# Second layer of a two-layer attention and expert kernel: two iterations to a block, six slots, and the experts after the fourth batch

## The reference

```python
xn = _layernorm(x)
q = (xn @ Mq).reshape(B, H, C, K)      # H = 8 heads, K = 64, C = 512
k = (xn @ Mk).reshape(B, H, C, K)
v = (xn @ Mv).reshape(B, H, C, V)      # V = 16
scores = einsum('bhqk,bhck->bhqc', q, k).reshape(B * H, C, C)
att = softmax(scores / sqrt(K), axis=1)            # over the queries
out = einsum('bqhc,bhcd->bqhd', att.reshape(B, C, H, C), v)
# gate: 8 experts, top 1: relu(x @ W1 + b1) @ W2 + b2
x = x + out * silu(experts(xn))
```

## Time and profile before

| | |
|---|---|
| Time, median of 3 runs | 820.05 us (819.98 to 820.12) |
| The profiled execution, its own time | 822.5 us |
| Its span | 820.8 us |
| PE busy (share of the span) | 736.7 us (90%) |
| DVE busy | 579.7 us (71%) |
| ACT busy | 380.4 us (46%) |
| POOL busy | 262.4 us (32%) |
| Second layer's bodies 0 and 1, with 32 scatters | 417.6 to 497.5 us of the span |
| Experts of the second layer | 497.5 to 588.0 us |
| Bodies 2 to 7 and the end | 588.0 to 820.8 us |

### The profile page before, as it was taken

One profiled execution on the slowest core, in us unless ns is written; L12 is line 12 of the kernel. 1 busy time (PEld: TensorE's weight loads), 2 busy tenths in 40 slices (PEclk: granted clock), 3 DMA queues, 4 the chain that ended last, 5 costly groups with the idle time before them and its releaser, 6 DMA issues.

```text
span 820.8 us, 20387 instructions
## 1 busy us (share of the span) xinstructions
PE 736.7 (90%) x6689; PEld 507.2 (62%) x6690; DVE 579.7 (71%) x1525; ACT 380.4 (46%) x922; POOL 262.4 (32%) x404
## 2 busy tenths in 40 slices
PE   5989889999999999994679898999999999999983
PEld 3667677888787787883334347888644444444431
DVE  5888864678777787787487684433587878878772
ACT  2333314444344344342045564444466667777772
POOL 7364200000000000000138743222122246676773
PEclk9999999999999999998599999999999999999996
DMA  8700000000000000000501101222100001111110
GB/s 248 229 0 0 1 1 1 1 1 0 0 0 0 0 0 0 0 0 0 147 15 43 40 21 35 59 58 58 37 2 2 2 15 28 28 28 32 37 33 20
DMA packets 34274, 25.06 MB, mean 31 GB/s; under 512 B 3303, under 2 KB 30626, under 8 KB 34210
## 3 DMA queue, kind: packets, MB, share of 16 engines
q1 hardware_dynamic: 31256, 19.48, 8.2%
q0 software_dynamic: 2048, 4.20, 1.8%
q10 hardware_dynamic: 906, 0.55, 0.3%
HBM read 14.91 MB, written 9.31 MB: 30 GB/s over the span
## 4 chain that ended last, share of the span: by engine, by line
PE 64%; DVE 16%; issue 9%; POOL 4%; ACT 2%; DMA 1%; DVEq 1%; POOLq 0%; ACTq 0%
PE bank L782 12%; PE bank L1345 11%; PE bank L766 9%; PE bank L1330 6%; PE bank L1304 5%; PE bank L1391 4%; PE bank L1400 4%; POOL vs L1256 2%; PE bank L450 1%; POOL xn_all L1270 1%; DVE vt L1533 1%; DMA xn_all<-y_sorted,slot_b 1%; PE bank L809 1%; PE bank L749 1%; DVE acc L1000 1%
## 5 line engine op out<-in xcount | busy, mean ns | idle before, releaser
L1454 ACT ACTIVATE pb<-bank,nmx 128x512 f32<-128x512 f32 x256 | 173.1, 682 | 76.2 <-DVE nmx L1587 73.2
L1587 DVE TENSOR_REDUCE nmx<-bank 128x2 f32<-128x1024 f32 x128 | 156.4, 1222 | 30.4 <-PE bank L1345 28.3
L1345 PE MATMUL bank<-qk 64*128 64x512 f32 x512 | 146.5, 649 | 12.7 <-ACT pb L1454 5.4
L853 ACT ACTIVATE hid<-bank,cols 128x512 f32<-128x512 f32 x128 | 87.9, 687 | 123.3 <-PE bank L766 123.2
L1256 POOL TENSOR_TENSOR vs<-vt,rz 128x256 f32<-128x256 f32 x128 | 78.7, 615 | 135.2 <-DVE rz L1563 120.2
L1330 PEld LDWEIGHTS bank<-pb,vs 128*32 128x32 f32 x2048 | 49.0, 110 | 104.0 <-issue 66.7
L782 PEld LDWEIGHTS bank<-w_e,hid 128*128 128x128 f32 x768 | 98.1, 191 | 8.3 <-DVE acc L1000 1.8
L782 PE MATMUL bank<-w_e,hid 128*128 128x128 f32 x768 | 100.2, 275 | 0.0
L728 POOL TENSOR_TENSOR r<-ve,half_neg 128x4 f32<-128x4 f32 x8 | 8.1, 1010 | 274.1 <-DVE ve L927 274.1
L1330 PE MATMUL bank<-pb,vs 128*32 128x128 f32 x2048 | 84.2, 283 | 6.0 <-POOL vs L1256 5.1
L1345 PEld LDWEIGHTS bank<-qk 64*128 64x128 f32 x512 | 39.3, 187 | 50.7 <-issue 24.3
(11 more groups left out here) (225 smaller groups left out, 1242.2 us busy)
## 6 DMA issues: line engine op xcount, KB each, us to landing
x_sorted<-zero SPq DMA_DIRECT2D x1, 2496.0 KB, 12.3
xn_all<-x_sorted SPq DMA_DIRECT2D x39, 64.0 KB, 1.8
y_sorted<-xn_all SPq DMA_DIRECT2D x39, 64.0 KB, 1.6
x_all<-in_L_attn_x_dram SPq DMA_DIRECT2D x8, 256.0 KB, 6.0
w<-in_L_ffn_W_dram SPq DMA_DIRECT2D x1, 2048.0 KB
out_dram<-xn_all SPq DMA_DIRECT2D x8, 256.0 KB
w_u<-in_L_ffn_ew_dram SPq DMA_DIRECT2D x1, 768.0 KB
w_e<-in_L_ffn_ew_dram SPq DMA_DIRECT2D x1, 768.0 KB
```

What stands on the lines that cost most here:

```text
L853: act.activation(hid[n % NU][:, :], psum[n % NU][:, :], ACT.Gelu, bias=col((ROW_AB1 if n < AC else ROW_EB1 - AC) + n), scale=1.0).then_inc ...
L1345: mm = pe.matmul(psum[score_banks(k) + ab], qk[bt % 2][half, 1, h, 2 * m:2 * m + 2, :].rearrange("p a k -> p (a k)"), qk[bt % 2][half, 0, ...
L1454: act.activation(pb[s + ab][:, :], psum[score_banks(k) + ab], ACT.Exp, bias=nmx[:, s + ab:s + ab + 1], scale=1.0, accum_out=zz[:, s + ab:s ...
L1587: dve.tensor_reduce(nmx[:, s:s + 2], banks[:, score_banks(k):score_banks(k) + 2, :], AX.X, ALU.max, negate=True).then_inc(n_mx, 1)
```

## The change

The line numbers in the changed kernel are up to 8 higher for DVE's lines. `LAG` goes from 3 to 4 and `SLOTS` from 4 to 6; the experts run after four bodies (`BEFORE` 4) and the scatters are spread over twice as many iterations; PE's body goes in blocks of two iterations: two scores, the mixed work of the even iteration, two values, the mixed work of the odd iteration. VAL moves from iteration 6 to 8, two PROJ from 11 and 15 to 10 and 13 (with 13 to 11). DVE stores an even iteration's mixed work after the next maximum and not ahead of it.

```diff
-        LAG = 3
-        SLOTS = 4
+        LAG = 4
+        SLOTS = 6
...
-        MIXED = {1: (PROJ, 0), 3: (PROJ, 1), 4: (TURN, 0), 5: (PROJ, 2), 6: (VAL, 0), 7: (PROJ, 3), 9: (PROJ, 4),
-                 11: (PROJ, 5), 12: (TURN, 1), 13: (PROJ, 6), 15: (PROJ, 7)}
+        MIXED = {1: (PROJ, 0), 3: (PROJ, 1), 4: (TURN, 0), 5: (PROJ, 2), 7: (PROJ, 3), 8: (VAL, 0), 9: (PROJ, 4),
+                 10: (PROJ, 5), 11: (PROJ, 6), 12: (TURN, 1), 13: (PROJ, 7)}
...
-        BEFORE = 2
+        BEFORE = 4
...
-                        for g in range(min(now * 3 // 4, NT), min((now + 1) * 3 // 4, NT)):
+                        for g in range(min(now * 3 // 8, NT), min((now + 1) * 3 // 8, NT)):
...
             def body(bt, kind, last):
-                for i in range(IT):
+                for i in range(0, IT, 2):
                     k = bt * IT + i
                     score(k)
+                    score(k + 1)
+                    mixed(bt, i)
                     if k >= LAG:
                         value(k - LAG)
...
+                        value(k + 1 - LAG)
+                    mixed(bt, i + 1)
...
-                    if i:
+                    if i and i % 2 == 0:
                         mixed(bt, i - 1)
                     if k > 1 and k not in (BEFORE * IT, BEFORE * IT + 1):
                         inverse(k - 2)
...
                     dve.tensor_reduce(nmx[:, s:s + 2], banks[:, score_banks(k):score_banks(k) + 2, :], AX.X, ALU.max,
                                       negate=True).then_inc(n_mx, 1)
+                    if i % 2:
+                        mixed(bt, i - 1)
                 mixed(bt, IT - 1)
```

More of the change, by code:

```diff
@@ L1157, in recurrent_d2_kernel @@
         mixed_bank = lambda u: psum[4 + u % 2] if u < FIRST_USES else psum[6]
-        values_in = lambda bt: 1 if bt == 0 else use_no[bt - 1, 6] + 1
-        pairs_in = lambda bt: FIRST_USES if bt == 0 else use_no[bt - 1, 15] + 1
+        values_in = lambda bt: 1 if bt == 0 else use_no[bt - 1, 8] + 1
+        pairs_in = lambda bt: FIRST_USES if bt == 0 else use_no[bt - 1, 13] + 1
         turn_use = lambda g: LAST_USE if g == 2 * B - 1 else use_no[(g // 2, 12) if g % 2 == 0 else (g // 2 + 1, 4)]
@@ L1355, in _, with mixed @@
                 project(mixed_bank(1 + g), g, 0)
+            def mixed(bt, i):
+                if (bt, i) in use_no:
+                    u = use_no[bt, i]
+                    what, num = MIXED[i]
+                    pe.wait_ge(mb_free, u)
+                    if what == PROJ:
+                        project(mixed_bank(u), num, bt + 1)
+                    elif what == VAL:
+                        v_part(mixed_bank(u), bt + 1)
+                    else:
+                        turn_heads(mixed_bank(u), bt * 2 - 1 + num)
             def body(bt, kind, last):
-                for i in range(IT):
+                for i in range(0, IT, 2):
                     k = bt * IT + i
                     score(k)
+                    score(k + 1)
+                    mixed(bt, i)
                     if k >= LAG:
                         value(k - LAG)
[L1363 to L1372, removed]
+                        value(k + 1 - LAG)
+                    mixed(bt, i + 1)
             def expert(k):
```

## The result

The changed kernel took 825.08 us (median of 4 runs, 823.85 to 826.75) and the kernel before 820.01 us (819.82 to 820.12): ratio 1.0062, 95% interval 1.0049 to 1.0074. It is slower by 5.1 us. The profiled execution of the changed kernel is the slowest of its four (826.75 us by its own time, span 825.1 us, against 822.5 and 820.8 before), so the spans are 4.3 us apart and not 5.1.

What follows compares the result with a forecast made beforehand. PE sets the pace, DVE 18% below it. Bodies +7.8 and -0.2, scatters -4.5, entering the experts +1.6, gathers +1.5, body 7 and the end 0: +6.2 us on 820.05, 826.2 us; range 817 to 833.

Steps and rivals of the forecast that it cites:

- The steady loss: Bodies without scatters: 38.0 us against 36.67, +1.3 each, from projections waiting for stores; +7.8 over bodies 1 to 6.
- Rival B: Whole kernel: no change or small gain, scatters' whole 6.5 us back and body 7 gaining 2 or more; 819 to 821, 18%.
- Light blocks: Blocks of iterations 0, 2, 6 with one projection at the end: 3.79 us each where such a pair took 4.14.
- Blocks 4 and 12: Blocks with TURN, then a projection: 5.89 us against 4.73 before, the projection waiting for copies behind the second maximum.
- rival A: Whole kernel faster: store waits do not bite, saved drains decide; a body 32.6 us, about 790 in all, 5%.
- Block 14: Block with nothing mixed: 2.93 us plus 0.14 as its second following score waits for exponentials, 3.07.
- Scatters: Bodies 0 and 1: half the density takes back 4.5 of 6.5 us lost, ends nothing and 6.5.
- Entering the experts: Last pair's first score to first transpose: 5.4 us after a block ending with late exponentials; +1.6 in the sum.
- Gathers: Joints of bodies 4 to 5, 5 to 6, 6 to 7: up to 0.7 us each, 0 to 2.1, taken as 1.5.
- The experts' phase: Experts, now two bodies later: phase and leaving stay the same, the later place costs nothing.
- Rival C: Whole kernel much slower: PE's shorter idles, four times in seven bodies, also lower its granted clock; +40 us, 4%.
- Body 7 and the end: No projections, so no store waits; PE 2 to 3 us faster but ACT waits for gathers: 0, ends -2 and +1.

Runs made afterwards that it cites:

- the first run: The changed kernel with every store on DVE ahead of the next maximum again; 810.98 us, ratio 0.9923.

## Why the prediction was right, point by point

The forecast was 826.2 us and slower; measured, 825.08. The steady loss came by the mechanism that was named, the wait for the bank behind the second maximum, and the first run undid it. That the sum came out at 825 is in good part luck. Against the span before, the changed trace is 4.3 us longer: 0.7 arose ahead of the second layer, where nothing was changed, +1.1 in bodies 0 to 6 with the entry to the experts, +0.95 in the experts, +1.5 in body 7 and the end. So the terms that the forecast had put at +6.2 came to little more than +1, and some 3 us arose where it had put nothing. Rival B, at 18%, had the sizes of the bodies better: the scatters came back whole. It missed at body 7, where it wanted a gain of 2.

- **Light blocks 3.79**: measured 3.79 and 3.80. **Two scores 0.86 apart**: 667.77 to 669.69 is 1.92 for both, as forecast. **Two values 0.43 apart**: the 0.90 from the first value to the projection behind both (662.11 to 663.01 in body 4's first block) is 0.43 + 0.46.
- **Blocks 4 and 12 at 5.89, 8 at 6.42, 10 at 5.37**: 5.75, 6.28, 5.25. Against blocks without a wait (4.38, 4.88 and 4.65, rival A's lengths) they lose 1.37, 1.40 and 0.60, where the forecast had 1.51, 1.54 and 0.72. The idle times in the rows (1.16, 1.20, 0.38, 1.17) are 0.2 shorter, since a row's duration reaches past the next row's start; 0.38 lies below the 0.7 to 1.5 that were to be seen. (That all four blocks lose 1 to 1.5 was loosely said even by the forecast's own sum, which has 0.7 for block 10.) The mis-sized step is the distance of two maxima with an inverse between them. I took 1.34 from the only such place, where the inverse had waited for ACT; in the steady state it is 1.21 (668.95 to 670.16). That is 0.13 in each of four blocks: a body is 37.5 and not 38.0, six bodies 4.9 and not 7.8. **Block 14 at 3.07** is right: 2.93 to the next score, and that pair of scores takes 2.14 instead of 1.99 (453.81).
- **Scatters, 4.5 of 6.5 taken back**: all of it, the second mis-sized term. Body 0 took 35.48, its clean length, and DVE shows no wait marked as remote in the changed trace. I had leant to this end and kept 2 us of it for late stores.
- **Entering the experts**: 5.4 forecast, 5.43 measured (563.33 to 568.76).
- **Gathers, 0 to 2.1 at three joints**: PE idles 1.20, 0.20 and 0.30 there, all ended by ACT's exponentials. With the later tanh the joints' idle times fell, which confirms the cause; that the bodies did not get shorter by it shows how little of it can be had.
- **The experts' phase "is the same"**: 0.95 longer. PE entered after an idle of 2.43, and its granted clock was 0.53 over the next 7.2 us:

```profile
568.76:576.00 7.24, 6.27 (x28) 5.81 (x29) 1.22 (x4) 1.97 (x7) 3.06 (x5) 0.53 0.10 28
```

In the kernel before the first 7.5 us of the phase had 0.77, after an idle of 1.53. The idle alone does not decide it: the run with the stores ahead has the same idle of 2.43, but 0.76 over its first 7.24 us, and its phase takes 90.38, like before (90.48). So the longer phase goes with the lower clock, and how low the clock fell at this place differs from run to run, which the forecast could not know. Rival C's mechanism exists here and in body 7; inside bodies 0 to 6 the clock stayed at 1.00 with idles of up to 1.41.
- **Body 7 and the end at 0** (ends -2 and +1): +1.5, outside. As I had it, PE ran ahead and then stood: 3.56 of idle until the exponentials behind the tanh, and the granted clock was 0.68 over the 10.7 us around it, so part of its work ran at 1.2 GHz. The kernel before has such a place too, an idle of 2.19 and then a score of 2.08 at 789.33, and its mean clock over body 7 and the end is 0.82 against 0.80. So the clock is only a little lower, but PE's busy time there is 32.89 against 33.00 although the work was paired. That a longer idle could eat the saved work this way I had left out; what else makes up the 1.5 was not taken apart.

```profile
792.00 2.08 PE L1345 MATMUL bank<-qk 64*128 64x512 f32 x4 [3.56 <-ACT pb L1460]
```

Rival A's price, 790 us, was that of the pairing with no store in the way. The version with VAL in the last block (ratio 0.9733, a body of 34.2 where rival A had 32.6) shows that about 22 of its 30 us can be had, with three more changes that the forecast did not consider. The rule of the Trainium skill ("TensorEngine Tiling (Array Packing)", Key Properties) that a change of tiling mode drains TensorE agrees with the trace: 0.20 and 0.15 us a change, and 2.5 us more busy time of PE a body in the run with the scores parted, which has 16 changes more in a body. It does not say whether the saving reaches the end.

## What to carry to other kernels

Grouping like matmuls saves the switches, but it also brings two jobs that share a buffer closer together: before grouping, walk one block with its longest chain (matmul, the consumer's queue ahead of the copy, the copy, next matmul), and put the copy ahead of anything in that queue that no one waits for sooner. An off-path engine can be the limit of a block all the same: DVE is busy 29.2 of 37.5 us here, and PE waits for it in four of eight blocks. Jobs that share a bank belong into blocks of their own; where one had such a block (VAL in the last one), its copy could stand behind the maximum without a wait on PE.

## What the runs showed of the hardware

- The length of one idle time of PE did not decide the granted clock. It stayed at 1.00 behind the 1.16 to 1.20 us that recur in the changed kernel's bodies, behind twelve of thirteen idles of 1.85 in the old order with the TURN's copies late, and there also behind one of 2.38 at 810.97. It fell behind the thirteenth of 1.85, behind 2.19 (789.33, before), 2.38 and 3.56 (792.00); a score then took up to 2.08 us instead of 1.13. At the experts' entry the first 7.24 us had 0.76 in one run and 0.53 in another after the same idle of 2.43, and with late experts alone 1.00 after 1.53.
- The experts' phase follows that clock: 88.90 us in the run that had 1.00 over its first 7.24 us, 89.8 to 90.9 in those with 0.76, 91.0 to 91.8 in those with 0.53 to 0.56.
- Stores marked as remote are not tied to dense scatters. Two stand in the trace of the later tanh and two in that of VAL in the last block, in bodies 5 and 6, beside gathers:

```profile
699.21 0.99 POOL L1270 DMA_INDIRECT xn_all<-y_sorted,slot_b  x1 [0.16 <-issue]
700.70 0.69 DVE L1545 COPY qk<-bank 128x512 f32<-128x512 f32 x1 [1.78 <-remote]
```

All seven (three before, four here) start 0.4 to 0.7 us after an indirect DMA on POOL has ended. Other stores run beside such DMAs and are not held up (the one at 667.96 in the changed kernel starts 0.5 us before a gather on POOL ends), so what held these up stays open. Dense scatters cost time without them too: PE waits 2.3 us for POOL's `vs` in bodies 0 and 1 of the changed kernel with `BEFORE = 2`.
